# Rows gathered in quarters and transposed on VectorE, and an expert's weights brought a quarter per block

## What is computed

```
y = down(silu(gate(x)) * up(x))            # W_gate, W_up (2752 x 1024), W_down, each + LoRA of rank 16
logits = y @ W_gate + b_gate               # 8 experts
_, top_idx = jax.lax.top_k(logits, 2)
y_all = jax.nn.relu(jnp.einsum('bsd,edh->bseh', y, W_e) + b_e)    # W_e: 8 x 1024 x 1024
return x + jnp.take_along_axis(y_all, top_idx[..., None], axis=2).mean(axis=2)
```

## Time and profile before

| | us |
|---|---|
| median of 3 runs | 1814.69 |
| lowest and highest | 1814.04, 1815.79 |
| span of the profiled execution | 1813.7 |
| PE busy in it | 1796.7 (99%) |
| DVE busy | 1249.1 (69%) |
| POOL busy | 1126.9 (62%) |
| ACT busy | 765.0 (42%) |

### The profile page before, as it was taken

How to read it: one execution, slowest core, us unless ns; L and a number is a source line. 1 busy time by engine, 2 the same in 40 slices (tenths; PEclk the granted TensorE clock), 3 DMA queues, 4 the chain that set the end, 5 groups by cost and what they waited for, 6 DMA issues and landing times.

```text
span 1813.7 us, 24875 instructions
## 1 busy us (share of the span) xinstructions
PE 1796.7 (99%) x8368; PEld 1495.5 (82%) x8368; DVE 1249.1 (69%) x1507; ACT 765.0 (42%) x1221; POOL 1126.9 (62%) x740
## 2 busy tenths in 40 slices
PE   9999999999999999999999999999999999999998
PEld 7788888888888888888888888888888888888886
DVE  8978888885569697888888876578698643234400
ACT  6544444444543336444444444543323333333343
POOL 2788888883444556556655553454545776777685
PEclk9999999999999999999999999999999999999999
DMA  6466666645577655555666555576636876567653
GB/s 236 160 231 223 211 206 218 235 157 185 179 245 255 221 180 200 180 171 181 203 203 212 193 196 193 191 252 226 224 117 195 247 193 155 141 185 196 153 100 53
DMA packets 129581, 349.27 MB, mean 193 GB/s; under 512 B 15393, under 2 KB 17313, under 8 KB 129185
## 3 DMA queue, kind: packets, MB, share of 16 engines
q1 hardware_dynamic: 110896, 286.94, 46.5%
q0 software_dynamic: 18560, 60.70, 14.3%
HBM read 266.44 MB, written 90.05 MB: 197 GB/s over the span
## 4 chain that ended last, share of the span: by engine, by line
PE 90%; DVE 5%; issue 2%; DMA 1%; ACT 1%; POOL 0%; SPq 0%; ACTq 0%; DVEq 0%; POOLq 0%
PE PS L1945 28%; PE PS L1946 27%; PE PS L1947 27%; PE PS L1994 2%; PE PS L2075 2%; PE PS L2307 2%; DVE R L1033 1%; DVE ring L1013 1%; PE PS L1980 1%; DVE FT L1453 1%; DMA FT<-y_scratch 0%; DVE FT L1466 0%; DVE FT L1316 0%; DMA FT<-in_xp 0%; PE PS L2219 0%
## 5 line engine op out<-in xcount | busy, mean ns | idle before, releaser
L1945 PE MATMUL PS<-R,ring 128*128 128x512 f32 (+1 forms) x1804 | 707.6, 392 | 5.4 <-DVE ring L1013 1.6
L1946 PE MATMUL PS<-R,ring 128*128 128x512 f32 (+1 forms) x1804 | 703.0, 390 | 0.0
L1947 PE MATMUL PS<-R,ring 128*128 128x512 f32 (+1 forms) x1804 | 702.5, 389 | 0.0
L1945 PEld LDWEIGHTS PS<-R,ring 128*128 128x128 f32 x1804 | 339.1, 188 | 74.2 <-issue 4.6
L1947 PEld LDWEIGHTS PS<-R,ring 128*128 128x128 f32 x1804 | 338.7, 188 | 71.7
L1946 PEld LDWEIGHTS PS<-R,ring 128*128 128x128 f32 x1804 | 339.1, 188 | 65.5
L846 POOL TENSOR_TENSOR ring<-raw,ring 128x1024 fp32r<-128x1024 f32 x70 | 175.3, 2504 | 214.9 <-ACT ring L1020 214.7
L824 POOL DMA_INDIRECT brw<-in_bgu,idx_b x88 | 99.5, 1131 | 216.5 <-DVE R L1203 185.5
L1945 PE MATMUL PS<-ring,R 128*128 128x512 f32 x592 | 231.0, 390 | 0.6 <-DVE R L1033 0.6
L1946 PE MATMUL PS<-ring,R 128*128 128x512 f32 x592 | 230.4, 389 | 0.0
L1947 PE MATMUL PS<-ring,R 128*128 128x512 f32 x592 | 230.3, 389 | 0.0
(11 more groups left out here) (205 smaller groups left out, 2421.8 us busy)
## 6 DMA issues: line engine op xcount, KB each, us to landing
raw<-in_wp SPq DMA_DIRECT2D x122, 512.0 KB
act_scratch<-FT SPq DMA_DIRECT2D x140, 256.0 KB
FT<-act_scratch SPq DMA_DIRECT2D x70, 512.0 KB, 4.5
raw<-in_we SPq DMA_DIRECT2D x64, 512.0 KB
ytp<-in_wgb SPq DMA_DIRECT2D x96, 256.0 KB
raw<-wt_scratch SPq DMA_DIRECT2D x40, 512.0 KB
out<-in_xn SPq DMA_DIRECT2D x17, 512.0 KB, 5.5
y_scratch<-FT SPq DMA_DIRECT2D x7, 1024.0 KB, 6.6
```

What stands on the lines that cost most here:

```text
L1945: e.matmul(out_, hi, whi, start=start, stop=False, skip_group_check=True)
L1946: e.matmul(out_, hi, wlo, start=False, stop=False, skip_group_check=True)
L1947: return e.matmul(out_, lo, whi, start=False, stop=stop, skip_group_check=True)
```

## The change

It does two things. The names are those of the diff.

**Rows.** From block `PB` = 3 on the eight transposes on TensorE are gone. `gather_quarters` issues four indirect transfers of 128 pieces of 1 KB, a quarter of a row each; their index `GQ` is made so that partition 32a+i of transfer g gets quarter a of row 32g+i. Then one VectorE instruction (`turn_rows`) transposes all 32x32 squares, which gives the numbers along the partitions, in the order in which partition m holds number 8m+k for product k; the weights' rows are loaded with a stride of 8 to fit. ScalarE makes the high part (`y_hi`) and VectorE the low part (`y_lo_v`). The ring of parts has three places in place of two. Blocks 0 to 2 keep their turns, with the same new order of the numbers.

**Weights.** Block c brings a quarter of the next expert: two pieces of 512 KB (`load_chunk`) and 256 columns of the bias (`load_quarter`). ScalarE makes the high parts (`chunk_hi`), VectorE the low parts (`chunk_lo`). Every expert gets at least four blocks (`ALU.max`), and `NB` becomes 56. From block 4 on the products wait for weights two units at a time.

With these, VectorE adds the bias straight from PSUM (`add_first`, `add_second`) in place of ScalarE's copy and GpSimd's add, and TensorE waits for these adds (`s_an0`, `s_an1`) in place of the copies (`s_zc`). `meta` moves and gets six parts, with more small instructions to write them. The diff, cut:

```diff
-NB = 41
+NB = 56
+LATE = 31
+PB = 3
...
             else:
-                src = we[a, b]
+                src = we_rows[bass.ds(1024 * a + b, 128, 8)]
...
+        def load_chunk(e, c, i):
+
+            n = C0 + 2 * c + i
+            if 2 * c + i < RW:
+                raw_free(e, n)
+            else:
+                e.wait_ge(s_el, 8 + 2 * c + i - RW + 1)
+            if c < 4:
+                src = we_rows[bass.ds(1024 + 2 * c + i, 128, 8)]
+            else:
+                row = e.value_load(meta[0:1, 3 * NB + c:3 * NB + c + 1], min_val=1024, max_val=1024 * 7 + 6)
+                src = we_rows[bass.ds(row + i, 128, 8)]
+            e.dma_start(raw_t(n), src).then_inc(s_raw[n % RW], 16)
...
+                at_c = e.value_load(meta[0:1, 5 * NB + c:5 * NB + c + 1], min_val=0, max_val=7 * 256)
+                row = e.value_load(meta[0:1, 4 * NB + c:4 * NB + c + 1], min_val=4, max_val=31)
+                e.wait_ge(s_an1, c - 1)
+                dst, src = AB[:, bass.ds(at_c, 256)], be_q[bass.ds(row, 1)]
+                src = src.rearrange("o n -> (o n)")
+            if c >= 2:
+                e.wait_ge(s_bi[c % 2], 16 * (c // 2))
+            e.dma_start(dst, src.partition_broadcast(128)).then_inc(s_bi[c % 2], 16)
...
             sp.run(e)
+            load_chunk(e, 0, 0)
+            load_chunk(e, 0, 1)
+            with ExitStack() as rest:
+                for b in range(NB):
+                    if b == 3:
+                        e.wait_ge(s_meta, 1)
+                        used = used_blocks(e)
+                    if b >= 32:
+                        rest.enter_context(e.If(used > b))
+                    if b + 1 < NB:
+                        load_chunk(e, b + 1, 0)
+                    load_quarter(e, b)
+                    if b + 1 < NB:
+                        load_chunk(e, b + 1, 1)
...
+        def gather_quarters(e, b):
+            if b == PB:
+                e.wait_ge(s_gq, 1)
+            if b == 5:
+                e.wait_ge(s_tp, 3)
+            if b >= PB + 3:
+                e.wait_ge(s_ty, b - PB - 2)
+            for g in range(4):
+                e.indirect_dma_start(out=ybuf[:, b % 3, g * 256:(g + 1) * 256], out_offset=None, in_=y_q,
+                                     in_offset=ioa(GQ[:, g, b:b + 1])).then_inc(s_gd[b % 3], 16)
...
+        def y_of(b):
+            return (brw if b % 2 else ytp)[:, :]
+
+        def turn_rows(e, b):
+
+            e.wait_ge(s_gd[b % 3], 64 * ((b - PB) // 3 + 1))
+            if b == 4:
+                e.wait_ge(s_tlo, 3)
+            e.transpose(y_of(b).rearrange("p (b g j) -> p g b j", g=4, j=32),
+                        ybuf[:, b % 3, :].rearrange("p (g i b) -> p g b i", g=4, b=8)).then_inc(s_ty, 1)
+
+        def y_hi(e, b):
+
+            e.wait_ge(s_ty, b - PB + 1)
+            e.wait_ge(s_blk, b - 1)
+            e.activation(ring_t(b, 0), y_of(b), ACT.Copy).then_inc(s_tc, 1)
+
+        def y_lo_v(e, b):
+
+            e.wait_ge(s_tc, b + 1)
+            e.tensor_tensor(ring_t(b, 1), y_of(b), ring_t(b, 0), ALU.subtract).then_inc(s_yv, 1)
+
+        def chunk_to(e, c):
+
+            if c < 4:
+                return 16384 + c * 4096
+            return e.value_load(meta[0:1, 2 * NB + c:2 * NB + c + 1], min_val=0, max_val=7 * 4096)
+
+        def chunk_t(at_c, i, part):
+            o = i * 2048 + part * 1024
+            return R[:, bass.ds(at_c + o, 1024)]
+
+        def chunk_hi(e, c, i, at_c):
+            n = C0 + 2 * c + i
+            arrived(e, n)
+            if c == 0:
+                e.wait_ge(s_z, 56)
+            if c >= 4:
+                e.wait_ge(s_k1, c - 3)
+            e.activation(chunk_t(at_c, i, 0), raw_t(n), ACT.Copy).then_inc(s_ch, 1)
+
+        def chunk_lo(e, c, i, at_c):
+            e.wait_ge(s_ch, 2 * c + i + 1)
+            e.tensor_tensor(chunk_t(at_c, i, 1), raw_t(C0 + 2 * c + i), chunk_t(at_c, i, 0), ALU.subtract).then_inc(s_el, 1)
...
+        def add_part(e, b, side, c0, n):
+            z = sbuf2[:, 2 * (b % 2) + c0 // 512, c0 % 512:c0 % 512 + n]
+            return e.tensor_tensor(z, PS[:, 4 + 2 * (b % 2) + c0 // 512, c0 % 512:c0 % 512 + n],
+                                   AB[:, bass.ds(side + c0, n)], ALU.add)
...
+            e.wait_ge(s_bl0, b + 1)
+            e.wait_ge(s_bi[b % 2], 16 * (b // 2 + 1))
+            e.wait_ge(s_bi[(b + 1) % 2], 16 * ((b - 1) // 2 + 1))
+            if b == 1:
+                e.wait_ge(s_bias, 16)
+            elif b < LATE + 2:
+                e.wait_ge(s_sc, 16 * (b - 1))
+            else:
+                e.wait_ge(s_sh, 16 * (b - LATE - 1))
+            add_part(e, b, side, 0, 512).then_inc(s_an0, 1)
+
+        def add_second(e, b, side):
+
+            e.wait_ge(s_blk, b + 2)
             if b >= 2:
                 e.wait_ge(s_sc, 16 * (b - 1))
...
             y_lo(e, 1)
             gather_y(e, 2)
-            add_bias(e, 0)
-            gather_y(e, 3)
+            add_bias0(e)
+            gather_quarters(e, 3)
             scatter(e, 0)
-            used = blocks_in_use(e)
-            for b in range(1, NB):
-                when(e, used, b + 1, y_lo, e, b + 1)
-                when(e, used, b + 3, gather_y, e, b + 3)
-                when(e, used, b, add_bias, e, b)
-                when(e, used, b, scatter, e, b)
-            whole = e.value_load(meta[0:1, 3 * NB + 6:3 * NB + 7], min_val=16 * 32, max_val=16 * NB)
-            halves = e.value_load(meta[0:1, 3 * NB + 8:3 * NB + 9], min_val=16, max_val=16 * (NB - LATE))
+            y_lo(e, 2)
+            gather_quarters(e, 4)
+            scatter(e, 1)
...
+                for b in range(2, NB):
+                    if b == 3:
+                        e.wait_ge(s_meta, 1)
+                        used = used_blocks(e)
+                    if b >= 3:
+                        clip_second(e, b - 1)
+                    if b >= 32:
+                        rest.enter_context(e.If(used > b))
+                    if b + 2 < NB:
+                        y_hi(e, b + 2)
+                    clip_first(e, b)
+                    if b + 1 < NB:
+                        at_c = chunk_to(e, b + 1)
+                        for i in range(2):
+                            chunk_hi(e, b + 1, i, at_c)
...
+            link(e.tensor_scalar(nb, nb, 4.0, None, ALU.max))
...
+            chunk_lo(e, 0, 0, chunk_to(e, 0))
             e.wait_ge(s_rk, 3)
...
+            pm, to_dump, rows = RT[:, 592:646], RT[:, 646:700], RT[:, 0:54]
+            link(e.tensor_copy(pm, PS[:, 1, 2:NB]))
+            link(e.tensor_tensor(pm, pm, PS[:, 1, NB + 2:2 * NB], ALU.add))
+            e.tensor_scalar(gidx[:, 2:3], pm[:, 0:1], -1.0, 0.0, ALU.add, ALU.max).then_inc(s_pm, 1)
+            link(e.tensor_scalar(rows, pm, -1.0, 0.0, ALU.add, ALU.max))
+            for g in range(4):
+                for a in range(4):
+                    m = e.tensor_scalar(GQ[32 * a:32 * a + 32, g, 3:NB], rows[32 * g:32 * g + 32, 1:54], 4.0, float(a),
+                                        ALU.mult, ALU.add)
+            m.then_inc(s_gq, 1)
...
+            link(e.tensor_scalar(part(5), un, 4.0, 256.0, ALU.add, ALU.mult))
+            link(e.tensor_scalar(part(1), side, 1024, None, ALU.mult))
...
+            chunk_lo(e, 0, 1, chunk_to(e, 0))
+            add_first(e, 1, 0)
+            add_second(e, 1, 0)
+            turn_rows(e, 3)
+            chunk_lo(e, 1, 0, chunk_to(e, 1))
+            y_lo_v(e, 3)
...
+            with ExitStack() as rest:
+                for b in range(2, NB):
+                    if b >= 3:
+                        add_second(e, b - 1, bias_side(e, b - 1))
+                    if b >= 32:
+                        rest.enter_context(e.If(used > b))
+                    if b + 2 < NB:
+                        turn_rows(e, b + 2)
+                    at_c = chunk_to(e, b)
+                    for i in range(2):
+                        chunk_lo(e, b, i, at_c)
+                    if b + 2 < NB:
+                        y_lo_v(e, b + 2)
+                    add_first(e, b, bias_side(e, b))
...
+                src = src.rearrange("p (m b) -> p b m", b=8)
...
                 for u in us:
                     n, k = divmod(u, 8)
-                    if u == 4:
+                    if b < PB and u == 4:
                         e.wait_ge(s_tc, b + 1)
                         e.wait_ge(s_tlo, b + 1)
+                    if b >= 4 and u < 8 and k % 2 == 0:
+                        e.wait_ge(s_el, 8 + 2 * (b - 3 + k // 2))
...
-
-            def begin(b, ready):
+                    if u == 9 and b >= 3:
+                        m.then_inc(s_k1, 1)
+
+            def begin(b):
+                if b >= PB:
+                    e.wait_ge(s_yv, b - PB + 1)
+                    return
                 if b:
...
+                off = e.value_load(meta[0:1, b:b + 1], min_val=0, max_val=16384) if b >= 4 else 0
+                begin(b)
+                if b == 2:
+                    e.wait_ge(s_zc, 2)
+                else:
```

(5 more changed lines are left out.)

298 lines of the change are left out of this document (146 added, 152 removed).

## The result

The changed kernel takes 1836.58 us (median of 4 runs, 1834.14 to 1841.3), the kernel before beside it 1814.45. The ratio of the times is 1.0125, 95% interval 1.0109 to 1.0141: it is slower by 22 us, where the forecast was 27 us faster. The profiled execution has a span of 1832.3 us, 18.6 above that of before.

A forecast was written before the change was run, and what follows sets the result against it. TensorE, busy for 99% of the span, was taken as the bound. Span 1813.7 - 30.3 (turns) + 4.7 (block 2) - 1.1 (end) = 1787.0, so time 1788.0 us; range 1780 to 1808.

The forecast's parts named there:

- What is removed: Blocks 3 to 36 lose TensorE's turn of eight transposes: 34 x 0.89 = 30.3 us off the path.
- What is added per block, beside TensorE: New per-block work on VectorE (6.3 us), ScalarE, GpSimd and DMA, each said to fit into 10.9 us.
- all of this is hidden: Added block work costs no time while each engine, and each ring of engines, takes under 10.9 us per block.
- The ring of engines: Dependency loop through GpSimd, VectorE and ScalarE, once round per two blocks: 12.5 us plus landing, taken as 3.5, against 21.8 available.
- a late VectorE: Case in the loop's sum: clip stands behind two ScalarE weight passes, 2.7 us more, 15.2 us plus landing per round.
- the ring binds: Rival: the engines' loop takes 24.1 us per two blocks, 12.05 per block, giving 1817 us; chance 0.12.
- half of it is possible too: 11.3 to 11.8 us per block: Rival in which the engines' loop binds in part, time 1792 to 1811 us; chance 0.08.
- The 10 us of slack: Rows and weight quarters ready early: some 10 us of lateness must pile up before TensorE stops in the blocks.
- Where the change costs: block 2: GpSimd's longer queue delays block 2's low parts: start 3.2 to 6.5 us later, 4.7 taken; half clock taken as 0.
- The end: After the last products, VectorE's add from PSUM replaces a copy and a GpSimd add: 1.1 us off.
- The new waits of TensorE: Rival: from block 4 on, waits for weights and adds cost 0.08 us each, 13 in all, 1801 us; chance 0.06.
- 37 blocks were used, as before: Answers a rival: experts under four blocks are filled up, adding blocks at 10.9 us each; called unlikely, no chance given.

The follow-up runs named there:

- the combined kernel: Changed kernel with bias load behind y stores, no rows for unused blocks, gathers ahead of scatter, first weight low part ahead of transpose: 1793.64 us, ratio 0.9878.

## Why the prediction was wrong

**What is removed** was right. With the ring open the period is 10.88 where it was 11.76: 0.88 for each turn, 0.89 in the sum.

**What is added per block, beside TensorE.** The loads were about right and the claim "all of this is hidden" failed. VectorE's transpose takes 2.14 us in the median, not 1.23. The sum for VectorE was 6.3 and is 7.1, within its bounds (5.7 to 7.5). The Trainium skill, "Vector Engine (DVE) Microarchitecture Reference", section 3.8, has it at one element per cycle per lane, an estimate of 1.07; the trace does not agree, and the measurement decides. No run here shows whether the width of the elements or the order in which they are read and written makes the difference. The quarters' gathers take 1.32 us each, inside the bounds. None of the engines is full. That was the trap: the step weighed engines one by one, and each of them had room.

**The ring of engines** is the step that failed. The ring was seen, but the forecast had the wrong way round it. It went from the transpose over splits and add straight to the clip, and for a late VectorE it put 2.7 us of two weight passes ahead of the clip on ScalarE. It left out what the second of these passes waits for: a load of 4.21 us, which waits for a `raw` buffer, which VectorE frees behind the same transpose. The four gathers took 10.3 us from the first issue to the transpose, where 4.0 + 3.5 was put in, and the load 4.21, where nothing was. So the round was 22.97 us, and not 16.0, nor the 18.7 of a late VectorE. The rival "the ring binds" was right that a ring would bind, and "half of it is possible too: 11.3 to 11.8 us per block" has the period; it had a chance of 0.20 in all, and TensorE's stops at the blocks, ended by the weight split, are what its signs named. But its ring was not the one that bound, for it has no weight load either. The experiment with the low part ahead of the transpose takes the load's link out, and one pass of 1.2 us with it; all else of the rival's ring stands, and the period falls to 10.92. The 10 us of slack that were to soften it are used up by block 5 and then help no more.

The Trainium skill, "DMA: Bandwidth & Descriptors", section Bandwidth, spoke for this rival with its rule on large transfers, and by the fixed cost that the page gives in its section on the anatomy of one DMA four quarters in a row were estimated at over 9 us. They take 10.4 in the median, and a whole gather 7.3: the number came out near, but the three transfers more cost 2 to 3 us in these runs and not 6, the estimate by that fixed cost.

**Where the change costs: block 2.** The kernel with the bias load put back has this stop without the first one. Block 2 starts there at 1397.43 us, 4.84 later than before, and 4.7 was taken. That it fits so well is in part luck. The index of gather 2 was to come some 2 us later and came 0.4 later (1382.78 in that run, 1382.40 before). The sixteen index writes were taken at 2.9 us, with up to 2.5 more if GpSimd's adds hold them up, and took 6.06: fifteen of them 0.18 each, and one 3.14, all through GpSimd's two adds. The two errors cancel, and the writes end at 1389.13, within the 1388 to 1390.4 of the sum. TensorE stood still for 4.85 us there and 5.59 in the changed kernel, where some 4 was expected; the half clock behind the stop, taken as 0 in a range of 0 to 2, was 1.8 us. Block 3 was called covered by 3 us and had a stop of 1.87. And the stop before block 0 was missed, 8.2 us at block 2: no part of the prediction speaks of `load_bias` and its new key. What SP issues in which order, row by row in both kernels, would have shown the bias load ahead of the stores and its wait on `s_ee`.

**The end** was forecast 1.1 us better and is 9.3 worse. With the ring open it is 8.3 to 9.8 us against the 9.4 of before, so no clear gain shows there either. Only the path of the data was followed (last product, add, clip, scatter), not what stands ahead of the add in VectorE's order: the transpose of a block that is not used, and its gather.

**The other rivals.** The new waits of TensorE cost nothing: with the ring open the period is that of the products. 37 blocks were used, as before.

## To carry over

When work is spread over engines that have room, add up each ring and not each engine: follow every in-order queue through all that stands ahead of the next link, a buffer that is freed and a load into it among it, and put a thing that others wait for ahead of a thing that waits. Where a schedule is set by keys, compare each queue's order row by row, the loads that seem untouched too, and follow the last iteration with its look-ahead by itself. When a ring binds, one reordering anywhere on it gives all of the gain and a second one nothing more.

## What the runs showed of the chip

- The 32x32 transpose of 128x1024 in float32 on VectorE takes 2.01 to 2.20 us, 2.1 ns for each element of a partition, in 36 instances, where one pass of a subtraction of that size takes 1.22.
- A write of 32x53 on VectorE took 0.18 us in fifteen cases of sixteen, no less than the 0.18 to 0.25 of 128x54. The sixteenth took 3.14 us, and GpSimd ran two adds of 1.29 us in that time.
- A stop of TensorE of 5.59 us was followed by four us at a granted clock of 0.50, one of 0.84 us by none. Stops of 3.6 to 3.9 us at one and the same place were followed by 8.8 to 9.3 us of it in the traces of four kernels and by 17.3 to 18.5 in those of four others.
- The issue of an indirect transfer on GpSimd took 0.94 us at best and up to 4.23 in the changed kernel; between 1430 and 1780 us its mean went from 1.35 us to 1.00 in the combined kernel, whose blocks do the same work in another order.
- Four gathers of 128 KB in pieces of 1 KB took 10.4 us in the median from the first issue to the transpose that waited for them, one of 512 KB in rows of 4 KB 7.3 (5.8 to 9.6).
